# Mixture layers: the pairs of gate weight rows are read back by indirect DMAs of GpSimd instead of spread reads of SyncE

## The reference

```python
nx = _rmsnorm(X, g2)
logits = xf @ Wr.T + expert_bias
rw = jax.nn.softmax(logits, axis=-1)
topw, topi = jax.lax.top_k(rw, TOP_K)
topw = jax.nn.softmax(topw, axis=-1)
combine = jnp.sum(jax.nn.one_hot(topi, NUM_EXPERTS, dtype=xf.dtype) * topw[..., None], axis=1)
shared = _swiglu(xf, sW1, sW2, sW3)
h = jax.nn.silu(jnp.einsum('td,efd->etf', xf, eW1)) * jnp.einsum('td,efd->etf', xf, eW3)
eo = jnp.einsum('etf,edf->etd', h, eW2)
specialist = jnp.einsum('te,etd->td', combine, eo)
```

## Time and profile before

| | |
|---|---|
| time, median of 3 runs | 2728.72 us (2727.49 to 2733.39) |
| the profiled execution: its time | 2731.78 us |
| the profiled execution: its span, first to last instruction | 2730.0 us |
| mean granted TensorE clock | 0.934 |
| busy: PE, DVE, POOL, ACT | 2443.1, 1947.8, 1487.3, 1378.8 us |
| `moe0` blocks, about | 450 to 650 and 962 to 1155 us |
| `moe1` blocks, about | 1552 to 1868 and 2405 to 2727 us |
| reads of pairs of rows | 64 in `moe0`, 64 in `moe1` |

### The profile page before, as it was taken

How to read it: one execution, slowest core, us unless ns; L and a number is a source line. 1 busy time by engine, 2 the same in 40 slices (tenths; PEclk the granted TensorE clock), 3 DMA queues, 4 the chain that set the end, 5 groups by cost and what they waited for, 6 DMA issues and landing times. The chain is left out here.

```text
span 2730.0 us, 39978 instructions
## 1 busy us (share of the span) xinstructions
PE 2443.1 (89%) x12716; PEld 1542.4 (56%) x12716; DVE 1947.8 (71%) x4454; ACT 1378.8 (51%) x2168; POOL 1487.3 (54%) x1371
## 2 busy tenths in 40 slices
PE   4477997998789989989999889998999999979998
PEld 3344565666656556644444467775444444347776
DVE  6865775775667667756666598886777778668887
ACT  4632453333435523256666445553777677645554
POOL 5924654443265534366666456655667566336654
PEclk8688898998869999989999999998999999789999
DMA  1001111221021032110000211110000000021221
GB/s 48 0 3 30 35 36 56 94 94 50 1 49 40 14 111 94 70 57 1 1 1 1 69 46 56 63 55 24 1 1 1 2 1 1 1 89 56 70 67 43
DMA packets 57512, 104.49 MB, mean 38 GB/s; under 512 B 15192, under 2 KB 30424, under 8 KB 57048
## 3 DMA queue, kind: packets, MB, share of 16 engines
q1 hardware_dynamic: 57304, 101.90, 11.7%
HBM read 86.53 MB, written 2.62 MB: 33 GB/s over the span
## 5 line engine op out<-in xcount | busy, mean ns | idle before, releaser
L2327 DVE TENSOR_REDUCE l_diffneg_max<-psum 128x1 fp32r<-128x512 f32 x512 | 336.0, 685 | 98.2 <-PE psum L2065 89.5
L4464 POOL TENSOR_TENSOR l_moe1sc<-l_moe1s,l_moe1bcs 128x512 f32<-128x512 f32 x192 | 276.5, 1453 | 218.1 <-ACT l_moe1s L4280 198.7
L2242 ACT ACTIVATE l_diffweights<-psum 128x1024 f32<-128x1024 f32 x256 | 261.7, 1025 | 142.3 <-PE psum L2094 141.4
L4280 ACT ACTIVATE l_moe1s<-psum 128x512 f32<-128x512 f32 x256 | 152.9, 598 | 231.5 <-PE psum L851 230.3
L2065 PE MATMUL psum<-l_diffkz,l_diffQ 128*128 128x512 f32 (+1 forms) x512 | 239.2, 486 | 2.9 <-DVE l_diffneg_max L2327 2.0
L4366 DVE TENSOR_TENSOR x<-l_moe1sc,psum 128x512 f32<-128x512 f32 x256 | 174.5, 682 | 89.2 <-POOL l_moe1sc L4464 60.0
L4373 DVE TENSOR_TENSOR l_moe1g_lo<-x,l_moe1g_hi 128x512 fp32r<-128x512 f32 x256 | 230.1, 900 | 0.1
L2866 ACT ACTIVATE l_lightswapped<-psum 32x512 f32<-32x512 f32 x304 | 178.7, 588 | 101.8 <-DVE l_lightturned L2958 98.3
L1592 DVE TENSOR_REDUCE l_attn0neg_max<-psum 128x1 fp32r<-128x512 f32 x256 | 167.3, 683 | 52.7 <-PE psum L1326 50.0
L173 POOL TENSOR_TENSOR settled<-powers 128x1 f32<-128x1 f32 x111 | 31.4, 283 | 302.4 <-DVE l_alibimv L698 72.0
L4280 ACT ACTIVATE l_moe0s<-psum 128x512 f32<-128x512 f32 x144 | 86.1, 598 | 211.7 <-PE psum L851 187.8
(11 more groups left out here) (583 smaller groups left out, 6749.5 us busy)
## 6 DMA issues: line engine op xcount, KB each, us to landing
l_moe0bcs<-gate_rows SPq DMA_DIRECT2D x64, 512.0 KB, 4.6
l_moe1bcs<-gate_rows SPq DMA_DIRECT2D x64, 512.0 KB, 3.8
l_attn0Q<-l_attn0q_hi SPq DMA_DIRECT2D x128, 64.0 KB, 2.0
l_moe1w_raw<-in_moe_w SPq DMA_DIRECT2D x20, 256.0 KB, 6.7
l_attn0Q<-l_attn0q_lo SPq DMA_DIRECT2D x64, 64.0 KB, 2.0
l_moe0w_raw<-in_moe_w SPq DMA_DIRECT2D x20, 128.0 KB, 5.1
x<-in_x SPq DMA_DIRECT2D x8, 256.0 KB, 4.5
out<-x SPq DMA_DIRECT2D x8, 256.0 KB, 2.3
```

The source lines that it names most:

```text
L2242: nc.scalar.activation(weights[:, tt, 2 * pair:2 * pair + 2, :], ps[:, S[m % 2]:S[m % 2] + 2, :], ACT.Exp, scale=SCALE).then_inc(act_exp.s ...
L2327: nc.vector.tensor_reduce(neg_max[:, n % 2, st, row:row + 1], ps[:, bank_of(("max", n, b)), :], AXX, ALU.max, negate=True).then_inc(vec_ma ...
L4280: nc.scalar.activation(s[:, n % 2, h, :], ps[:, H1[(n * HT + h) % 2], :], ACT.Silu).then_inc(act_silu.sem, act_silu.step("silu", h))
L4464: nc.gpsimd.tensor_tensor(sc[:, n % 2, h, :], s[:, n % 2, h, :], weights_row(n), ALU.mult).then_inc(pool_sc.sem, pool_sc.step("sc", h))
```

## The change

SP no longer reads the rows. POOL does, with an indirect DMA for each pair: the rows of a sequence are seen as four rows of 1024 numbers, and each of the 128 partitions has the number of the row that it is to get in `row_of`, which POOL fills once per block with `iota` (so all partitions name the same row). The rows of each sequence get a DRAM tensor of their own. A pair k is asked for in POOL's program where slot k - 2 is done, behind that slot's scaling; it waits for the use of the rows it replaces (k - 6, k - 5), and at a new sequence for the store of its rows.

```diff
+        PAIRS_OF_ROWS = moe.experts // 2
+        row_of, rows_numbered = sb("row_of", [P, PAIRS_OF_ROWS], U32), core_semaphore(nc, name + "_rows_numbered")
...
-            def spread_rows(j, experts):
-                for e in experts[::2]:
...
             for g in range(weights_in.groups):
-                spread_rows(0, range(2 * g, min(2 * g + 2, ROWS)))
                 weights_in.sync_group(sp, g)
...
-            spread_rows(0, range(ROWS, moe.experts))
             for j in range(1, NSEQ):
                 chooser.store_rows(sp, j)
-                sp.wait_ge(chooser.rows_stored, 16 * j)
-                spread_rows(j, range(moe.experts))
...
+            def spread_rows(k):
+                if k >= ROWS:
+                    for m in (k - ROWS, k - ROWS + 1):
+                        j, e = divmod(m, moe.experts)
+                        for h in range(HT):
+                            scaling_done(p, j * NE + e + moe.shared, h)
+                if k >= moe.experts:
+                    p.wait_ge(chooser.rows_stored, 16 * (k // moe.experts))
+                if k == 0:
+                    p.wait_ge(rows_numbered, 1)
+                j, e = divmod(k, moe.experts)
+                pairs_of_rows = core.dram["gate_rows"][j].rearrange("(f two) t -> f (two t)", two=2)
+                p.indirect_dma_start(bcs[:, k % ROWS:k % ROWS + 2, :].rearrange("p e t -> p (e t)"), None, pairs_of_rows,
+                                     bass.IndirectOffsetOnAxis(ap=row_of[:, e // 2:e // 2 + 1], axis=0)).then_inc(row_loaded[k % ROWS // 2], 16)
+
+            nc.gpsimd.iota(row_of[:, :], [[1, PAIRS_OF_ROWS]], 0, 0).then_inc(rows_numbered, 1)
+            spread_rows(0)
             token_scale(1)
...
                         scale_slot(n, h)
+                if e >= moe.shared and rowed(n) % 2 == 0 and rowed(n) + 2 < NSEQ * moe.experts:
+                    spread_rows(rowed(n) + 2)
                 if e == 0 and add_to is not None:
...
-        dram["gate_rows"] = nc.dram_tensor("gate_rows", (NSEQ, 8, T), F32, kind="Internal").ap()
+        dram["gate_rows"] = [nc.dram_tensor(f"gate_rows{j}", (8, T), F32, kind="Internal").ap() for j in range(NSEQ)]
```

More of the change, by code:

```diff
@@ L4143, in _ @@
         def _(sp):
-            def spread_rows(j, experts):
-                for e in experts[::2]:
-                    k = rowed(j * NE + moe.shared + e)
-                    if k >= ROWS:
-                        for m in (k - ROWS, k - ROWS + 1):
-                            j_, e_ = divmod(m, moe.experts)
-                            for h in range(HT):
-                                scaling_done(sp, j_ * NE + e_ + moe.shared, h)
-                    two = core.dram["gate_rows"][j, e:e + 2, :].rearrange("e t -> (e t)").unsqueeze(0).to_broadcast([P, 2 * T])
-                    sp.dma_start(bcs[:, k % ROWS:k % ROWS + 2, :].rearrange("p e t -> p (e t)"), two).then_inc(row_loaded[k % ROWS // 2], 16)
             tokens = core.dram["out"].rearrange("b (q p) d -> p (b q) d", p=P)
```

## The result

The changed kernel takes **2769.95 us** (median of 4 runs, 2757.81 to 2773.6) against 2730.56 us for the kernel before (4 runs, same chip): ratio 1.0138, 95% interval 1.0117 to 1.0159, so 38 us slower. The forecast was 2748.2 us, +19.5. The profiled execution happens to be the lowest of the four: time 2757.81 us, span 2756.0 us, clock 0.939. Its `diff` block, which the change does not touch, lasted 517.0 us against 526.8 in the profile of before, and between 516 and 533 us over all kernels of this study. Two spans therefore cannot be subtracted here. I compare blocks and sequences instead, from the start of PE's turning of the combined weights (L235), called C, to the next C.

What follows compares the result with a forecast made beforehand. PE was taken to set the pace of the mixtures; 3.9 + 13.3 + 7.3 + 3.0 - 8.0 = +19.5 us gave 2751.3 us for the profiled execution and 2748.2 us for the median, range 2721 to 2803 us.

Steps and rivals of the forecast that it cites:

- Part 1: Cost of a gather: it holds POOL for 1.0 us, and its rows land 4.2 us after its start.
- Part 2: Tokens behind the store in moe0: PE waits 0.07 us in ten sequences, longer in two late ones; +3.9 us.
- Part 3: Rows 4 and 5 gathered behind POOL's power in moe0: PE waits 0.95 us in each sequence; +13.3 us.
- Part 4: Next block's first tokens, once per moe0: POOL's chain behind the gather, PE waits 3.6 us; +7.3 us, lower clock +3.0.
- Part 5: Starts of four blocks: weights come 2 us earlier as fewer reads stand ahead of them; -8 us, bounds 0 and -14.
- Part 6: Gathers between moe1's scalings fit into POOL's idle 1.39 and 1.11 us; costs nothing up to a G of 1.1.
- One index at a time: Rival: software takes indices singly, a gather holds POOL 5.44 us and POOL becomes the bound; 2858 us or more, chance 0.05.
- Starved descriptors: Rival: POOL and DVE hinder each other, a gather holds POOL 2.5 us; +74 us, 2803 us, chance 0.15.

Runs made afterwards that it cites:

- e5: The change with plain DMAs of POOL, the row broadcast to all partitions, in place of the indirect ones; ratio 1.0075 to the kernel before.
- e7: The kernel before plus, in moe0, a POOL iota ahead of the tokens that waits for the store, SP still reading the rows; ratio 1.0010.
- e1: The change, but in moe0 the gather of the next sequence's rows 0 and 1 stands behind the tokens in POOL's program; ratio 1.0115 to the kernel before.
- e8: The change, but in moe0 SP reads rows 0 and 1 of each sequence from the second on; 2748.83 us, ratio 1.0084 to the kernel before.
- e12: The kernel before, but after each store in moe0 SP reads rows 0 and 1 behind rows 2 to 5, without gathers; ratio 1.0122.
- e3: The change with the edits of e1 and e2 together; 2732.49 us, ratio 1.0010 to the kernel before.
- e14: e3 with DVE's h_lo of the next sequence moved to slot 0, ahead of the scaling of slot 1; ratio 0.9996 to the kernel before.
- e15: The kernel before, but at the start of moe0 SP asks for rows 2 to 5 behind all weight loads, without gathers; ratio 0.9973.
- e10: The change in moe1 alone, moe0 reading its rows by SP; ratio 1.0024 to the kernel before.
- e9: e8 with moe0's gather of rows 4 and 5 moved to slot 1, ahead of the power; ratio 0.9993 to the kernel before.
- e2: The change, but in moe0 the gather of rows 4 and 5 is issued in slot 1, not behind the power; ratio 1.0086 to the kernel before.
- e11: The good places of e3 with plain DMAs of POOL in place of indirect ones; ratio 1.0008 to the kernel before.

## Why the prediction was wrong

The direction, the places and G were right; the size was half.

**Part 1.** G, the time that a gather holds POOL: 1.0 us taken, 1.0 to 1.1 measured in `moe0`, 1.26 in `moe1`. L, from its start to the landed rows: 4.2 taken, 4.45 to 4.55 measured. The Trainium skill's fit for a DMA issued by GpSimd (DMA: Bandwidth & Descriptors, Anatomy of one DMA — SWDGE) gave 3.2 us; the plain DMA of e5 took 4.0 us (median of its profile's page) and the indirect one more, so for this transfer the fit is too short, and by it the wait behind the power would have been missed.

**Part 2 is the step that failed.** It let the gather begin at C + 2.78, as SP's read did, so that ten sequences wait 0.07 us. POOL does see the store about then (C + 2.89 in e7), but the indirect DMA begins 0.68 us after that. With 0.1 us more of G the turning came 0.95 us late in every sequence: 11.4 us for twelve, against the 3.9 of the forecast, its two late stores included. (That is the lateness and not its price: e1 took it away and got back 0.43 us a sequence.)

**Part 3 was mis-sized by the same 0.8 us.** "Rows 0 and 1 are asked for at C + 2.78 as before" was the sentence that failed. They were used 1.04 us late, the power began 1.0 us late, and the gather behind it at C + 18.67 where the working had C + 17.55. The lateness of slot 5 was 3.16 us against the 1.8 forecast; 0.79 us of DVE's slack covers part (1.13 less a hand-over of 0.34), which leaves the 2.4 us of the whole period. I had priced parts 2 and 3 as two separate delays of 0.07 and 0.95; they are one chain from the store, where tokens and rows 0 and 1 are late side by side (0.97 us at PE) and the power's gather adds 1.43. That it is one chain is shown by e8; that its single cuts do not add is shown by e1 and e12, where `h_lo` behind slot 1 takes over. The forecast had no such second path.

**Part 4** held, term by term. 7.3 + 3.0 us were forecast and 10.5 measured from the seventh C to the end. The waits at L472 are 3.58 and 3.96 us, together 7.5, and the 2.9 us left go with the 3.4 us at a granted clock of 0.50 behind each (one such stretch alone cost 1.6 us at the same place in the first block of e1, 30.5 against 28.9). Rows 0 and 1 of the last sequence, late too, have no part: in e3 and e14 slot 1 is 0.7 to 2.0 us late there, and the end takes 28.9 us as before.

**Part 5** was right for `moe0` (2.0 us a block taken, the logits came 2.7 and 2.4 us earlier, e15 shows the gain alone) and wrong for `moe1`, where it took another 4 us. In the first `moe1` ACT's first weights came 7.6 us after the start in place of 6.2. In the second they came 4.1 us after it in place of 6.3, as forecast, and yet the first C came 1.1 us later; why is open. In `moe0` the clock may have a share that the working left out: from the start to the logits the granted clock was 0.50 for 13.9 and 10.0 us before, and for 5.4 and 7.4 us in the change.

**Part 6**, "Nothing", is 3 to 11 us by e10's interval, starts of `moe1` included. It looked at a middle sequence and at POOL's idle time of 1.1 to 1.4 us; the end, where the opening chain leaves POOL none, was not read.

**The sum again**, in the pieces of the result, forecast against measured. The twelve periods: 11.4 + 3.9 = 15.3 against 27.6, which is 12 x 2.40 less 1.2 us of late stores that the periods of before already held. From the seventh C to the end: 10.3 against 10.5. From the start of `moe0` to the first C: -4 + 1.9 = -2.1 against -1.6 (-5.1 at the logits, +3.5 from there on; rows 4 and 5 are late there too, and the clock was at 0.50 for 1.4 and 2.1 us against 2.8 and 0; the shares are not known). `moe1`: -4 against +0.3. In all 19.5 against 36.8. Twelve of the seventeen missing microseconds are the chain, four are `moe1`.

**The rivals.** One index at a time is out: 1.0 us for 128 indices. The Trainium skill's 102 cycles for an index (GPSIMD Engine Reference, Performance pitfalls for Q7 kernels), by which I estimated 5.4 us, do not describe this DMA. Starved descriptors, at G = 2.5, did not come about; its total of +74 was far off, and in `moe0` of the change DVE's scaling never lasted longer than 0.75 us.

## What to carry over

A wait inserted in an in-order engine delays everything that this engine makes next, and what those products feed may be the next insertion's own start: follow the delay once around the loop rather than price each place by itself. A DMA on a compute engine belongs where its data are wanted late and its engine is idle: in `moe0` the gathers cost 38 us in the change (27.6 + 10.5), and in e14, with all of them indirect and one step of DVE moved besides, the median period is that of before. The only gain came from what stood ahead of the first weights, and needed no new engine (e15); after an edit of this kind, ask which half of it pays, and keep that.

## What was not expected of the hardware

- **A DMA of POOL has a lead time of its own.** Released by the store at C + 2.89, the indirect one begins at C + 3.54 to 3.57 and the plain one at C + 3.3. In e8 the addition ends at C + 3.04 and the gather still begins at C + 3.58, while behind work that ends later the gap is 0.16 to 0.19 us: behind the power, and behind an addition in e9 (order of time):

```profile
555.21 1.74 POOL L4470 TENSOR_TENSOR x<-x 128x512 f32<-128x512 f32 x1
...
557.13 1.34 POOL L4484 DMA_INDIRECT l_moe0bcs<-gate_rows,l_moe0row_of  x1 [0.18 <-issue]
```

So the lead time runs beside the engine's earlier work and shows only behind a semaphore wait. That the sequencer spends it on preparing the DMA is my reading; no run looked inside.

- **Indirection costs about 0.4 us of POOL and 0.45 us of landing** for 128 descriptors of 4 KB (e5 against the change).
- **Three 512 KB reads asked for within 0.9 us land one after another**: 4.0, 4.8 and 5.6 us after their issues (medians of e12; one alone 3.5).
- **A DVE instruction beside a gather can be stretched.** In e3, 4 of the 128 scalings of `moe0` took over 2 us in place of 0.69, 7 in e14, 1 each in e2 (3.6 us) and e11, none in the change or in e9. The one in the sequence read lies beside the end of a gather and POOL's addition behind it (e3, order of time):

```profile
549.89 1.10 POOL L4471 DMA_INDIRECT l_moe0bcs<-gate_rows,l_moe0row_of  x1 [0.77 <-DVE l_moe0sc L4339]
...
550.37 2.50 DVE L4339 TENSOR_TENSOR l_moe0sc<-l_moe0s,l_moe0bcs 128x512 f32<-128x512 f32 x1
```

With seven of them e14 is at 23.31 us, so they cost PE little or nothing; their cause stays open.
